# Two-layer cross attention: layer-1 keys and values per batch, with set-up loads and moves in other places

## The reference

```python
# layer 0 (mask: 1 keeps, 0 drops)
q = x @ Wq0.T + bq0;  k = ctx @ Wk0.T + bk0;  v = ctx @ Wv0.T + bv0
p = softmax(where(mask == 0, -1e9, q @ k.T))
x1 = p @ v + x
# layer 1
Q = x1 @ Wq1.T + bq1;  K = ctx @ Wk1.T + bk1;  V = ctx @ Wv1.T + bv1     # 16 heads
A = softmax(Q @ K.T / sqrt(32));  o = (A @ V) @ Wo.T + bo
out = layernorm(o + x1) * gamma + beta
```

## Time and profile before

| | |
|---|---|
| median of 3 runs | 407.41 us (405.67 to 409.12) |
| profiled execution | 406.01 us, of which the span of the trace is 404.2 us |
| TensorE busy | 381.1 us, 94% |
| VectorE, ScalarE, GpSimd busy | 73%, 61%, 55% |
| DMA | 42.51 MB, mean 105 GB/s |

### The profile page before, as it was taken

How to read it: one execution, slowest core, us unless ns; L and a number is a source line. 1 busy time by engine, 2 the same in 40 slices (tenths; PEclk the granted TensorE clock), 3 DMA queues, 4 the chain that set the end, 5 groups by cost and what they waited for, 6 DMA issues and landing times.

```text
span 404.2 us, 11980 instructions
## 1 busy us (share of the span) xinstructions
PE 381.1 (94%) x4860; PEld 288.4 (71%) x4860; DVE 294.9 (73%) x711; ACT 245.0 (61%) x749; POOL 222.3 (55%) x245
## 2 busy tenths in 40 slices
PE   8999878689999999999999999999999999899894
PEld 8968755457777777778776777777777777677663
DVE  0455349356886699679976899779967996658786
ACT  2333657267557855786658665885578567865820
POOL 0520338323565775478647765776657854773541
PEclk9999989699999999999999999999999999999998
DMA  8786014040005222242215212522252221622022
GB/s 311 286 327 209 14 24 119 20 150 26 11 17 170 78 95 69 79 171 96 69 43 182 92 42 59 177 76 85 71 170 79 95 69 33 198 96 69 17 105 104
DMA packets 20822, 42.51 MB, mean 105 GB/s; under 512 B 2942, under 2 KB 4478, under 8 KB 19744
## 3 DMA queue, kind: packets, MB, share of 16 engines
q1 hardware_dynamic: 20336, 41.21, 30.3%
q10 hardware_dynamic: 432, 0.54, 0.4%
HBM read 26.49 MB, written 8.39 MB: 86 GB/s over the span
## 4 chain that ended last, share of the span: by engine, by line
PE 80%; DMA 9%; ACT 4%; DVE 4%; SPq 1%; issue 1%; DVEq 0%
PE ps_q L1018 22%; PE ps_out L1104 20%; PE ps_t L1046 10%; PE ps_pv L1079 7%; PE ps_s L1032 7%; DMA p_b<-p_a 5%; PE ps_out L978 5%; DMA pt<-pt 3%; ACT prob L547 2%; PE ps_s L1122 1%; PE ps_s L944 1%; PE ps_s L957 1%; SPq L290 1%; DMA raw<-in_w0k 1%; ACT pt L558 1%
## 5 line engine op out<-in xcount | busy, mean ns | idle before, releaser
L404 POOL TENSOR_TENSOR prob<-prob,rc 128x308 f32<-128x308 f32 x128 | 91.6, 722 | 123.5 <-DVE rc L772 122.8
L547 ACT ACTIVATE prob<-ps_s,mx 128x77 f32<-128x77 f32 x512 | 120.0, 332 | 2.4 <-DVE mx L763 2.2
L558 ACT ACTIVATE pt<-ps_t 128x512 f32<-128x512 f32 (+2 forms) x93 | 55.5, 597 | 60.3 <-PE ps_t L1046 57.2
L770 DVE TENSOR_REDUCE sm<-prob 128x4 f32<-128x308 f32 x128 | 59.5, 465 | 32.5 <-ACT prob L547 32.1
L763 DVE TENSOR_REDUCE mx<-ps_s 128x4 f32<-128x308 f32 x128 | 53.8, 466 | 23.9 <-PE ps_s L1032 23.9
L1046 PE MATMUL ps_t<-ident,prob 128*128 128x128 f32 (+1 forms) x372 | 58.9, 281 | 5.5 <-DMA v<-v 3.5
L1046 PEld LDWEIGHTS ps_t<-ident,prob 128*128 128x128 f32 (+1 forms) x372 | 46.5, 154 | 16.8 <-issue 7.4
L378 POOL TENSOR_TENSOR x_l<-x_raw,x_h 128x512 fp32r<-128x512 f32 x32 | 44.7, 1400 | 20.9 <-ACT x_h L493 10.7
L1018 PE MATMUL ps_q<-x_h,wq_h 128*128 128x512 f32 x128 | 54.5, 426 | 0.0
L1018 PE MATMUL ps_q<-x_h,wq_l 128*128 128x512 f32 x128 | 53.7, 419 | 0.0
L578 ACT ACTIVATE ct_h<-ps_pv 128x512 fp32r<-128x512 f32 x32 | 19.1, 597 | 47.6 <-PE ps_pv L1079 47.5
(11 more groups left out here) (134 smaller groups left out, 618.9 us busy)
## 6 DMA issues: line engine op xcount, KB each, us to landing
x_raw<-in_xT SPq DMA_DIRECT2D x8, 1024.0 KB, 6.6
y<-in_x SPq DMA_DIRECT2D x28, 256.0 KB, 3.1
out<-y SPq DMA_DIRECT2D x28, 256.0 KB, 2.8
pt<-pt SPq DMA_DIRECT2D x31, 102.0 KB
pt<-pt SPq DMA_DIRECT2D x31, 52.0 KB
mask_sb<-in_mask SPq DMA_DIRECT2D x8, 154.0 KB, 6.4
raw<-in_w0q SPq DMA_DIRECT2D x4, 256.0 KB, 5.3
raw<-in_w0v SPq DMA_DIRECT2D x1, 1024.0 KB, 9.7
```

Of the source, the lines that this page charges most:

```text
L404: nc.gpsimd.tensor_tensor(ap, ap, wide(rc[:, k % 2, h], KEYS), ALU.mult).then_inc(prob_done, 1)
L547: e = nc.scalar.activation(prob[:, k % 2, t, h], ps_s[:, h, t * KEYS:(t + 1) * KEYS], ACT.Exp, bias=mx[:, k % 2, h, t:t + 1])
L558: nc.scalar.activation(pt[0:n, c], ps_t[0:n, :], ACT.Copy).then_inc(pt_ready, 1)
L770: nc.vector.reduce_sum(sm[:, k % 2, h], prob[:, k % 2, :, h], AX_X).then_inc(sum_done, 1)
```

## The change

Keys and values of layer 1 are projected one batch at a time, by `project_one`, with 128x77 matmuls. Batch 0 stays in the set-up and step 0: its keys are split into 12 matmuls ahead of the first `fold` and 4 at the old place; its values into 8 and 8, and their transposes stand behind `layer0` of step 0. Batch 1 goes through `ps_out`: values after the first transposes of step 2, their transposes in step 3, keys in step 3 between the 10th and the 11th matmul of the query, where `ps_out` must first be emptied (`v1_ready`). `scores` of unit 4 waits for `k1T_ready` of batch 1.

The wait for the moved values goes from the start of step 1 to `context` of units 0 and 4, one for each batch. On SyncE w1k and w1v lose one wait each. The x load is split into two halves of 512 KB. In the steady state the first half stands behind the gathers of g = 2, and the second half and the mask stand ahead of the gathers and `p0` moves of g = 3. The first such load (block 1) stands behind the moves of `u` instead of ahead of them. The first `p0` move is issued by ScalarE. The `y` loads leave step 1 for steps 3 and 4. ScalarE copies w1o before the query of step 0 instead of after it, GpSimd takes the rests of w1o at the ends of steps 0 and 3, and VectorE rounds half of block 1's x in step 0 instead of step 1. Some buffers change place in SBUF.

```diff
+        ctxT_sb = sb("ctxT_sb", [P, CH, BATCH * KEYS])
+        raw3 = sb("raw3", [P, CH, DIM])
+        v1T = sb("v1T", [P, BATCH, CH, KEYS])
...
             sp.wait_ge(mm_k0T, CH)
-            sp.wait_ge(l0_done, 1)
...
-            sp.wait_ge(mm_v0T, 2)
...
-            def next_inputs(i, b):
+            def next_x(i, b, first, last):
...
                 j = i + (b + 1) // 2
-                wait(sp, xl_ready, CH * blocks(i, b + 1))
+                wait(sp, xl_ready, CH * blocks(i, b) + last)
+                wait(sp, l0_done, blocks(i, b + 1))
+                sp.dma_start(x_raw[:, first:last].rearrange("p c t -> p (c t)"),
+                             xT[(b + 1) % 2, j, :, first * BLOCK:last * BLOCK]).then_inc(ld_xT, 16)
+
+            def next_mask(i, b):
+
...
                 wait(sp, sel0_done, blocks(i, b + 1))
-                sp.dma_start(x_raw[:].rearrange("p c t -> p (c t)"), xT[(b + 1) % 2, j]).then_inc(ld_xT, 16)
                 sp.dma_start(mask_sb[:].rearrange("p t k -> p (t k)"), mask[(b + 1) % 2, j]).then_inc(ld_mask, 16)
             def load_rows(i, b, t):
...
-            next_inputs(0, 0)
             stack_weights(u_a, u_b, slice(0, 1), u_stacked[0], u_ready, 1)
-            stack_probs(0, 0)
+            next_x(0, 0, 0, 2)
+            next_x(0, 0, 2, CH)
+            next_mask(0, 0)
...
-            sp.wait_ge(v1_ready, BATCH)
             by_heads = v1[:].rearrange("p b (g h d) -> p b g h d", h=GROUP_HEADS, d=HEAD_DIM)
-            for v in range(BATCH):
-                sp.dma_start(v1_2[SHIFT:SHIFTED, v], by_heads[:, v, :, 2]).then_inc(v1_moved, 16)
+
+            def move_values(v):
+
+                sp.wait_ge(v1_ready, v + 1)
+                sp.dma_start(v1_2[SHIFT:SHIFTED, v], by_heads[:, v, :, 2]).then_inc(v1_moved[v], 16)
+
+            move_values(0)
...
             def step(i, k):
                 g, b = k % CH, k // CH
+                if g == 3:
+                    next_x(i, b + 1, 2, CH)
+                    next_mask(i, b + 1)
                 gather(i, k - 1, 0)
                 if g == 3:
                     stack_probs(i, b + 1)
                 gather(i, k - 1, 1)
                 if k == 1:
                     stack_weights(u_a, u_b, slice(1, 2), u_stacked[1], u_ready, 2)
+                if k == 3:
                     sp.wait_ge(mm_u, BATCH)
                     sp.wait_ge(wq_ready, 2)
                     sp.wait_ge(wq_l_ready, 2)
-                    for t in range(TILES):
+                    load_rows(i, 0, 0)
+                if g == 2:
+                    next_x(i, b + 1, 0, 2)
+                if g == 3:
+                    store(i, b - 1, 0)
+                if k == 4:
+                    move_values(1)
+                    for t in range(1, TILES):
                         load_rows(i, 0, t)
-                if g == 3:
-                    next_inputs(i, b + 1)
-                    store(i, b - 1, 0)
                 if g == 3 and b == LAST - 1:
                     sp.wait_ge(xl_ready, CH * BLOCKS)
                     sp.wait_ge(xh_ready, CH * BLOCKS)
...
-                if type(i) is int and k == 1:
-                    wo_rest(0)
...
-                if type(i) is int and k == 1:
-                    wo_rest(1)
...
-                if type(i) is int and k == 1:
+                if k == 0:
+                    wo_rest(0)
+                    wo_rest(1)
                     wo_rest(2)
+                if k == 3:
                     wo_rest(3)
...
+            def leave_one(src, made, to, bias, ready, v, scale=1.0):
+
+                act.wait_ge(made, v + 1)
+                for c in range(CH):
+                    left = nc.scalar.activation(to(c), src[:, c * KEYS:(c + 1) * KEYS], ACT.Identity, bias=bias[:, c:c + 1], scale=scale)
+                left.then_inc(ready, 1)
+
+            def leave_v1(v):
+
+                act.wait_ge(mm_v1, v + 1)
+                nc.scalar.activation(v1[:, v], (ps_pv, ps_out)[v][0:KEYS, :], ACT.Copy).then_inc(v1_ready, 1)
...
+            act.wait_ge(p0h_ready, 1)
+            act.dma_start(f32(p0_a[KEYS:P, 0]), f32(p0_a[0:TAIL, 0])).then_inc(p0_stacked, 16)
+            act.dma_start(f32(p0_b[KEYS:BROWS, 0]), f32(p0_a[TAIL:KEYS, 0])).then_inc(p0_stacked, 16)
             act.wait_ge(bk1_ready, 1)
-            leave(bank[1:3], mm_k1T, k1T, bk1_scaled, k1T_ready, scale=SCALE)
+            leave_one(bank[1], mm_k1T, lambda c: k1T[:, c, 0:KEYS], bk1_scaled, k1T_ready, 0, scale=SCALE)
...
-                    leave(bank[5:7], mm_v1T, v1T, cols_sb[:, 5], v1T_ready, first=0, last=2)
+                    leave_one(bank[5], mm_v1T, lambda c: v1T[:, 0, c], cols_sb[:, 5], v1T_ready, 0)
...
-                if k == 0:
-                    leave(bank[5:7], mm_v1T, v1T, cols_sb[:, 5], v1T_ready, first=2, last=CH)
+                if k == 2:
+                    leave_one(ps_out, mm_v1T, lambda c: v1T[:, 1, c], cols_sb[:, 5], v1T_ready, 1)
+                if k == 3:
+                    leave_v1(1)
...
+                if k == 0:
+                    leave_v1(0)
+                    act.wait_ge(ld_w1o, 16)
+                    for c in range(CH):
+                        nc.scalar.activation(wo_h[:, c], raw3[:, c], ACT.Copy).then_inc(wo_h_ready, 1)
...
                 round_q(i, k + 1)
+                if k == 3:
+                    leave_one(ps_out, mm_k1T, lambda c: k1T[:, c, KEYS:2 * KEYS], bk1_scaled, k1T_ready, 1, scale=SCALE)
...
-                wait(pe, ld_xT, 16 * (blocks(i, b) + 1))
+                wait(pe, ld_xT, 32 * blocks(i, b) + 16)
...
+                if b == 2:
+                    pe.wait_ge(k1T_ready, 2)
...
-                if g == 1:
+                if g == 1 and k > 1:
                     layer0_negative(i, b + 1)
                     layer0_mask(i, b + 1)
...
+                if k == 0:
+                    layer0_negative(i, b + 1)
+                    layer0_mask(i, b + 1)
+                    round_x(i, b + 1, 0, 2)
...
+            def project_one(to, weights, v, made, loaded, first=0, last=CH):
+
+                pe.wait_ge(loaded, 16)
+                for e in range(first, last):
+                    for c in range(CH):
+                        mm = nc.tensor.matmul(to[:, e * KEYS:(e + 1) * KEYS], weights[:, c, e * P:(e + 1) * P],
+                                              ctxT_sb[:, c, v * KEYS:(v + 1) * KEYS], start=(c == 0), stop=(c == CH - 1))
+                if last == CH:
+                    mm.then_inc(made, 1)
...
                 wait(pe, exp_done, heads(i, k, 0))
+                if k == CH:
+                    pe.wait_ge(k1T_ready, 2)
...
+                if k == 0:
+                    pe.wait_ge(v1_zero, 1)
+                    pe.wait_ge(v1_moved[0], 16)
+                if k == CH:
+                    pe.wait_ge(v1_moved[1], 16)
...
+            project_one(bank[1], raw0, 0, mm_k1T, ld_w1k, 0, 3)
             pe.wait_ge(ld_w1q, 16)
...
-            project(bank[1:3], raw0, ctxT_sb, mm_k1T, [ld_w1k, ld_w1k])
+            project_one(bank[1], raw0, 0, mm_k1T, ld_w1k, 3, CH)
             pe.wait_ge(u_stacked[0], 32)
             pe.wait_ge(u_copied, 1)
             query(0, 0, 3 * CH, QUERY)
             pe.wait_ge(u_ready, 1)
-            project(bank[5:7], raw1, ctxT_sb, mm_v1T, [ld_w1v, ld_w1v], 0, 1)
-            pe.wait_ge(k1T_ready, CH)
+            project_one(bank[5], raw1, 0, mm_v1T, ld_w1v, 0, 2)
+            pe.wait_ge(k1T_ready, 1)
...
                 if k == 0:
-                    project(bank[5:7], raw1, ctxT_sb, mm_v1T, [ld_w1v, ld_w1v], 1, CH)
+                    project_one(bank[5], raw1, 0, mm_v1T, ld_w1v, 2, CH)
                     layer0(i, b + 1)
+                    pe.wait_ge(v1T_ready, 1)
+                    to_rows(ps_pv, v1T[:, 0], 0, mm_v1)
                 if type(i) is int and k == 1:
-                    pe.wait_ge(v1_ready, BATCH)
-                    pe.wait_ge(v1_zero, 1)
-                    pe.wait_ge(v1_moved, 32)
+                    pe.wait_ge(v1_ready, 1)
                 transposes(i, k - 1, 0)
+                if k == 2:
+                    pe.wait_ge(u_ready, BATCH)
+                    project_one(ps_out, raw1, 1, mm_v1T, ld_w1v)
                 if g == 3:
                     part(0)
                     transpose0(i, b + 1)
+                if k == 3:
+                    pe.wait_ge(v1T_ready, 2)
+                    to_rows(ps_out, v1T[:, 1], 0, mm_v1)
                 query(i, k + 1, 0, 5)
...
-                if k == 0:
-                    pe.wait_ge(v1T_ready, CH)
-                    for v in range(BATCH):
-                        to_rows(bank[5 + v], v1T, v, mm_v1)
...
                 elif g == 3:
                     part(2)
+                    if k == 3:
+                        pe.wait_ge(v1_ready, BATCH)
+                        project_one(ps_out, raw0, 1, mm_k1T, ld_w1k)
                     query(i, k + 1, 10, QUERY)
```

(9 more changed lines are left out.)

21 lines of the change are left out of this document (10 added, 11 removed).

## The result

The changed kernel took 416.22 us (median of 4 runs, 415.23 to 416.71) where the kernel before took 408.26 us beside it (405.67 to 409.33): a ratio of 1.0201, 95% interval 1.0145 to 1.0257, so it is slower by 1.5 to 2.6%. The forecast of 404.1 us and its range to 408.5 both missed. The profiled execution has a span of 413.3 us, against 404.2.

A forecast was written before the change was run, and what follows sets the result against it. TensorE, busy 94% of the span, was taken as the bound, with gains only before about 95 us. Unit 4 4.3 us earlier, steady state +1.0: -3.3 on 406.0 gives 402.7, or 404.1 us by the median; range 397.5 to 408.5.

The forecast's parts named there:

- the stop in the set-up: Set-up, stacked query: TensorE waits some 2.2 us for the p0 move, taken to land 4.5 us behind the last issue.
- A new stop costs the clock: Rival: new stops in set-up or unit 3 bring one lower-clock stretch of 1.7 to 3.0 us; 407.1 us, chance 0.13.
- The wait for `ps_out`: Unit 3: the keys wait 2.1 us until ScalarE empties the bank behind the unit's last exponentials.
- the wait for the keys: Unit 3, behind context: the next scores wait 0.75 us for the copies of k1T, queued behind q on ScalarE.
- the bare work: Unit 3: 7.3 us left of 11.3 after removing slow clock and two waits, 0.8 of it for a copy.
- stops of 1.1 us left the clock high: Argument on the clock rival: in the earlier trace stops of 1.1 us kept the clock, those of 3.5 did not.
- P: Layer-1 projections: assumed time of 16 matmuls of the split, 3.4 us, with ends of 2.35 and 4.4.
- the rival of cheap narrow matmuls: Layer-1 projections: 16 matmuls take only 2.35 us, 3.9 us less in total, 400.2 us; chance 0.30.
- the value wait: Unit 1: the 3.45 us wait for moved values and 1.7 us of slow clock go, -5.15 us.
- the stop did not move to `context`: Rival: unit 1's stop only moves to context of unit 0, 5.15 us come back, 409.3 us; chance 0.05.
- the gather that I had in mind: Unit 2: waits of 0.6 to 2.1 us for the gather's path, taken as 1.4, in a unit of 11.6 us.
- the steady state: Blocks behind the start: x and mask ahead of the p0 moves cost 0.2 us in each of 5 blocks, +1.0 us.

The follow-up runs named there:

- experiment 2: Changed kernel with 16 dummy 128x512 matmuls where TensorE stops in the set-up: 413.55 us, ratio 1.0167 to the kernel before.
- experiment 6: Changed kernel with 12 extra unused 128x512 matmuls right behind the stacked query matmuls: 417.63 us, ratio 1.0202 to the kernel before.
- experiment 1: Changed kernel with all 16 key matmuls of batch 0 behind the transposes of v0, none ahead of the first fold: 411.83 us, ratio 1.0136.
- experiment 10: Changed kernel with batch 0's value matmuls moved behind unit 0's scores and unit 1's whole query, nothing added: 420.17 us, ratio 1.0218.
- experiment 5: Changed kernel with set-up transfers in old order: block 1's x and mask ahead of the u moves, p0 move on SyncE: 417.71 us, ratio 1.0209.
- experiment 7: Changed kernel with the steady-state x load and mask back behind the stacking moves: 416.65 us, ratio 1.0196.
- experiment 3: Kernel before with only the wait for the moved values put at the context of unit 0: 400.54 us, ratio 0.9857.
- experiment 12: Kernel before with only the moved-values wait put at unit 0's context, run again with more rounds: 403.93 us, ratio 0.9854.
- experiment 4: Changed kernel with ScalarE's copy of batch 1's values placed right behind the rounding of p0 in step 3: 413.46 us, ratio 1.0161.
- experiment 11: Kernel before with the value wait at unit 0's context and layer-1 key and value matmuls split into 77 columns in place: 406.66 us, ratio 0.9935.
- the two repairs: Edits to the changed kernel: batch 0's key matmuls behind v0's transposes, and batch 1's value copy earlier; together 407.32 us, ratio 0.9980.
- experiment 9: Changed kernel with all batch 0 key matmuls behind v0's transposes and batch 1's value copy earlier: 407.32 us, ratio 0.9980.

## Why the prediction was wrong

**The step that failed: the stop in the set-up, and the clock behind it.** The forecast saw that TensorE would wait at the stacked query, for "some 2.2 us instead of 0.67", and gave it no cost beyond its own length. It was 3.8 us. It began at 33.9 us for 33.4, since the fold came 2.1 us later than before and not 1.75; it ended at 37.70 for 35.65, since the last move was issued 0.5 us later than assumed and landed 6.0 us after that, not 4.5. So 2.05 of the 8.0 us by which unit 1 was late are the landing. The clock behind it took 5.5 to 5.9: the windows give 5.9, and the same rows in experiments 2 and 6, at the full clock, are 5.5 us shorter in all. Experiments 1 and 2 remove the stretch in two unlike ways and get 3.4 and 4.5 us back at unit 1, net of the later start of the one and of the pauses in `layer0`.

**Why the clock's share was priced too low.** The rival "A new stop costs the clock" named the right mechanism with 0.13 and 407.1 us. It took 1.7 to 3.0 us for one stretch from the earlier trace rows. Those rows show about 6 us of low clock, but the work behind those stops held queries of 512 columns. The forecast itself put narrow key, value and layer-0 matmuls behind its new stop, and did not ask whether that changes the price. Experiments 6 and 10 show the size: 6.1 and 6.6 us of low clock with wide matmuls behind the stop, 12.9 with narrow ones. And it allowed one stretch, where there were two. The sign of being wrong that it named, a clock under 0.9 between 33 and 45 us or in unit 3, came in both places.

**Unit 3: the stop was foreseen, its clock not.** The wait for `ps_out` was forecast at 2.1 us and is 1.70; the wait for the keys at 0.75 and is 0.47. What was missing is the clock: 3.4 us by the window, 2.9 against unit 3 at the full clock (14.78 us, experiment 1). The other 0.8 us is the wait for a copy of transposed probabilities, which the forecast took out of the bare work and which is still there (0.78 us, at 82.31). The argument "stops of 1.1 us left the clock high" was used for stops longer than that. Here the outcome is not even fixed by the stop: it was 1.69 or 1.70 us long in seven of the kernels run, and the clock fell behind it in five (the changed kernel, 2, 5, 6, 7) and stayed at 1.00 in two (1, 10). Nor does a longer stop settle it. Two traces of one kernel, experiments 3 and 12, stop for `p_b` in unit 3 like this:

```profile
79.25 0.50 PE L1018 MATMUL ps_q<-p_a,u_a 128*128 128x512 f32 x1 [1.69 <-DMA p_b<-p_a]
...
79.73 0.50 PE L1018 MATMUL ps_q<-p_a,u_a 128*128 128x512 f32 x1 [2.31 <-DMA p_b<-p_a]
```

The first row is of experiment 3: behind the shorter stop the mean clock is 0.59 up to 83 us. The second is of experiment 12: behind the longer stop it stays at 1.00. So experiments 1 and 4 do not show that their edits decided unit 3's clock: in 4 the stop was gone, in 1 it stood and the clock stayed up all the same. What tells the cases apart I can't say.

**Right: the price of the split.** P was forecast at 3.4 us, by the weight loads. It is 3.49 us in unit 2, and 7.06 for twice the group in experiment 11. The Trainium skill's rule for loads ("TensorE: Matmul & The Clock Gate", section "LDWEIGHTS (loading the stationary operand)", columns divided by 1.2, in ns) gives 0.107 us a record; the traces show 0.109 and 0.110. So the rival of cheap narrow matmuls, to which 0.30 went, is out.

**Right: the value wait.** Unit 1 came out at 10.03 us for 9.97, and the stop did not move to `context`. In the kernel before, the edit alone gains 1.5%, some 6 us (experiments 3 and 12). Of that unit 1 gives 4.0 us, for the 5.15 forecast in the changed kernel, and unit 2 most of the rest. Unit 2 of the changed kernel was 0.6 us longer than forecast: its waits are a copy (0.78) and the q behind the copies of `v1T` on ScalarE (0.91), not the gather that I had in mind.

**Right in the number, perhaps by luck: the steady state,** +1.0 us forecast and measured. The mechanism is right only in part: the `p_b` waits did double from 0.5 to 1.0 us, but taking them away (experiment 7) gained nothing, and others with the same steady state needed 1 to 5 us more ("Left open").

**The account.** At unit 4 the kernels stand at 81.4 (experiment 12), 86.7 (split in place), 85.1 (the changed kernel without its two stops) and 95.2 us (the changed kernel). Splitting costs 5.3 us; the new places of the work may give back 1.6 of it, which is less than the 2.0 to 2.6 us by which single traces differ; and what the two repairs take away, the stops and their clock, costs 10.2. The change also contains the gain of 5.8 us that the value wait alone brings at unit 4 (87.15 to 81.4). What the runs support for this kernel is that edit without the split.

**Left open.** From unit 4 to the end the changed kernel needs 318.1 us, but experiments 1, 2, 5, 6 and 10, with no edit there, need 321.4 to 323.3, and 4 and 9 need 319.1 and 319.9. It is why most repairs moved the total less than unit 4. The first five have more waits for `p_b` (1.6 to 3.1 us for 1.0) and one gather wait of 1.8 to 3.0 us near 360 us, and behind that a third stretch of lower clock. It is the 8 in the page of experiment 1:

```profile
PEclk9999999999999999999999999999999999989999
```

In windows of 5 us around it the missing clock adds up to 1.4 to 1.7 us in each of the five. In the changed kernel and in 4, 7 and 9 the gather wait is 0.6 to 1.6 us long and the clock behind it 1.00. Why the gather comes late in some kernels I did not test, and each has one trace.

## What to carry to other kernels

Price a new stop of TensorE by its length plus the clock behind it: here, behind stops of 3.7 to 3.8 us, 3 us more when wide matmuls followed, 6 when only narrow ones did. Behind stops of 1.7 to 2.4 us it was nothing in some traces and 1.5 to 3.4 us in others. Work issued behind a transfer's issue is cover for it, and work placed ahead of it only delays it, so look at which side of the issue an edit puts its matmuls. Splitting a matmul until its columns take less time than its weight load doubles the loads and saves nothing on them: here 7.06 us for 4.37.

## What the hardware did that I had not expected

- The same narrow matmuls ran at 1.00 when nothing stopped ahead of them (experiments 2 and 11, and 66.78 us above) and at a mean of 0.54 for 12.9 us behind a stop of 3.8 us. The work is the same; what stood ahead of it differs.
- 12 extra wide matmuls, 5.2 us of work, moved the start of unit 1 by 0.01 us.
- A stop of 1.7 us was followed by the lower level in five kernels and not in two, and in two traces of one kernel a stop of 1.69 us was followed by it and one of 2.31 us was not.
- The move of `p0` landed earlier (36.65 for 37.46 us) when it was issued later (32.59 for 31.44), from SyncE's queue and with the x load put in front of it.
